# A 256-step recurrence on TensorE and ScalarE: the four block products of every second step in another order

## The chip, the cores and the metric

The kernel runs on one core of one Trainium2 chip. The metric is the device time of one execution in microseconds (us). TensorE (PE) multiplies, and its weight loads are a row of their own in the profile (PEld); ScalarE (ACT) evaluates tanh; VectorE (DVE) prepares inputs and adds outputs; SyncE's queue (SP) issues most transfers.

## What is computed

Two layers on x of 32 sequences, 256 steps and 256 features. In the first the transform and its inverse cancel up to a gate, so that the kernel computes x1 = x * (2 + gate). The second is a plain recurrence, and it is where the time goes:

```
h = silu(q_pool @ W1.T + b1);  gate = sigmoid(h @ W2.T + b2)
x = x + (v + a)                      # = x * (2 + gate)
next_h = tanh(prev_h @ Wh + xw)      # xw = x @ Wx + b, 256 steps in turn
x = x + h_t
```

Each step needs the whole h of the step before it: 256 features for 32 sequences.

## The kernel before

**Layout.** Features lie on the partitions, in two halves of 128. A step's argument z has half 0 and half 1, called m in the code; the h of the step before has half 0 and half 1, called k. z half m is bias + Wx part + sum over k of Wh[k, m] * h[k]. One step's recurrent work is thus four blocks (k, m): `recur(s, k, m, h)`. Each is issued by `by_columns` as four products on 32 columns of the array; a float32 product becomes two weight loads and two matmuls, so that a block is 8 of each in the trace.

**Names in the trace.** z half 0 lies in the tensors `bank_e`, half 1 in `bank_l`. A row `bank_e<-h_ring,wh_sb` is therefore block (0,0) or (1,0), and `bank_l<-h_ring,wh_sb` is block (0,1) or (1,1). In the text they are called e0, e1 (h half 0 and 1 into z half 0) and l0, l1 (into z half 1).

**Loop.** `TURN` is four steps; 64 turns run on PE with steps s = 0 to 3. Loop step s reads h of ring slot s and makes z of slot (s+1) mod 4. Before the four blocks of a step, `fill(s, turn)` issues work that does not need h: bias and input products for steps ahead (nothing at s = 0; at the others rows of the tiles `ones,b_sb` and `x_ring,wx_sb`). Everything on PE is issued in the order written; waits stand in that order too.

**Handshakes.** PE waits for `h_ready[s][k]` before the first block that reads h half k. The last matmul of block (1, m) increments `z_whole[m]`. ScalarE waits for `z_whole[0]`, writes tanh of half 0 into `h_ring`, then waits for `z_whole[1]` and does half 1 (line 178). In every second step it also waits for an output addition (`out_ready`) of long before. VectorE waits for h half 1 (`h_ready[..][1]`), adds outputs and scales the next inputs (`input_ready`), for which `fill` waits.

Of the kernel before, what the change touches and what calls it, by code (L numbers as in the profile page):

```python
# [14 lines left out]
def build(nc, x, x_first, w1_cond, w2, wx, wh, b_rows, out):  # L15
    CHUNKS, HALVES, N = x.shape[1:]
    D = HALVES * P
    B = w1_cond.shape[2] - D - 2
# [5 lines left out]
    TURN, PART = 4, 2  # L24
# [3 lines left out]
    with ExitStack() as ctx:  # L28
        def sb(name, shape, dt=F32):
            return ctx.enter_context(nc.sbuf_tensor(name, shape, dt))  # L30

        def sem(name):
            return ctx.enter_context(nc.semaphore(name))
# [30 lines left out]
        h_ring = sb("h_ring", [P, HALVES, TURN * B])  # L64
# [20 lines left out]
        def z_of(s, m, steps=1):  # L85
            part, of = divmod(s, PART)
            return bank_l[part][of][:, 0:B] if m else bank_e[part][:, of * B:(of + steps) * B]
# [23 lines left out]
        z_whole = [sem(f"z_whole_{m}") for m in range(HALVES)]  # L111

        h_ready = [[sem(f"h_ready_{s}{m}") for m in range(HALVES)] for s in range(TURN)]
# [68 lines left out]
        def _(pe):  # L182
# [8 lines left out]
            def by_columns(out, weights, moving, start=False, stop=False, columns=32):  # L191
                for q in range(0, P, columns):
                    done = nc.tensor.matmul(out[q:q + columns], weights[:, q:q + columns], moving,  # L193
                                            start=start, stop=stop, skip_group_check=True)
                return done
# [5 lines left out]
            def gate_product(layer, k, m, w_t, operand):  # L201
                return by_columns(z_ps[layer][m], w_t[:, k, m * P:(m + 1) * P], operand[:, k, :],
                                  start=(k == 0), stop=(k == HALVES - 1), columns=64)
# [11 lines left out]
            def lay_input(s, steps, k, m, columns=32):  # L215
                return by_columns(z_of(s, m, steps), wx_sb[:, k, m * P:(m + 1) * P],
                                  x_ring[:, k, s * B:(s + steps) * B], columns=columns)


            def recur(s, k, m, h, columns=32):  # L220
                return by_columns(z_of(s, m), wh_sb[:, k, m * P:(m + 1) * P], h, stop=(k == HALVES - 1),
                                  columns=columns)
# [8 lines left out]
            for m in range(HALVES):  # L231
                for k in range(HALVES):
                    if m == 0:
                        pe.wait_ge(w1_loaded[k], DMA)
                    done = gate_product(0, k, m, w1_t, cond_t)
                done.then_inc(z1_product, 1)
            keep_warm(1)
            for k in range(HALVES):
# [3 lines left out]
                for m in range(HALVES):  # L242
                    done = gate_product(1, k, m, w2_t, silu)
# [12 lines left out]
            for k in range(HALVES):  # L256
# [3 lines left out]
                for m in range(HALVES):  # L260
                    done = lay_input(0, 1 if m else 2, k, m, columns=64)
# [9 lines left out]
            def fill(s, turn):  # L271
                if s == 1:
                    pe.wait_ge(input_ready[1], turn)
                    for m in range(HALVES):
                        lay_bias(2, 2 - m, m)
                        lay_input(2, 2 - m, 0, m)
                        lay_input(2, 2 - m, 1, m)
                if s == 2:
                    lay_bias(3, 1, 1)
                    lay_input(3, 1, 0, 1)  # L280
                    lay_input(3, 1, 1, 1)
                    lay_bias(0, 2, 0)
                    pe.wait_ge(input_ready[0], turn)
                    lay_input(0, 2, 0, 0)
                if s == 3:
                    lay_input(0, 2, 1, 0)
                    for at in range(PART):
                        lay_bias(at, 1, 1)
                        lay_input(at, 1, 0, 1)
                        lay_input(at, 1, 1, 1)  # L290
# [10 lines left out]
            with nc.Fori(1, TURNS + 1, engines=only_pe, head_slot={pe.engine: 6}) as turn:  # L301
                for s in range(TURN):
                    fill(s, turn)
                    for k in range(HALVES):
                        pe.wait_ge(h_ready[s][k], turn)
                        for m in range(HALVES):
                            done = recur((s + 1) % TURN, k, m, h_ring[:, k, s * B:(s + 1) * B])
                            if k == HALVES - 1:
                                done.then_inc(z_whole[m], 1)

        @block.vector
        def _(dve):
# [124 lines left out]
```

## Time and profile before

| what | value |
|---|---|
| median of 3 runs | 197.54 us (197.27 to 198.22) |
| profiled execution, own time | 197.27 us |
| its span, first to last instruction | 195.3 us |
| outside the span | 1.97 us |
| granted TensorE clock over the span | 1.000 |

The profiled execution is the lowest of the three. Starts in the timeline are given to 0.01 us. The end of a matmul is a modelled value; starts of weight loads and of activations are recorded.

### The profile page before, as it was taken

The numbers are of one execution on the slowest core, as the hardware profiler recorded it, in microseconds if no ns is written. First come the engines' busy times: TensorE is split into PE (matmuls) and PEld (weight loads), VectorE is DVE, ScalarE is ACT, GpSimd is POOL, SyncE is SP. The second block draws the span as 40 slices with busy tenths as digits, with TensorE's granted clock in tenths as the row PEclk, the third lists the DMA queues.
The fourth block names the chain that finished last, engine by engine and source line by source line (L and its number), as shares of the span: only waits on it lengthen the run. The fifth ranks groups of instructions, "written<-read, shape, count | busy, mean of one in ns | idle before, by whom it ended". The sixth has DMA issues, their size and how long they took to land.

```text
span 195.3 us, 33383 instructions
## 1 busy us (share of the span) xinstructions
PE 176.3 (90%) x15962; PEld 164.9 (84%) x15962; DVE 97.3 (50%) x395; ACT 76.8 (39%) x518; POOL 0.5 (0%) x5
## 2 busy tenths in 40 slices
PE   5799999999999999999999999999999999999995
PEld 3788898898888889889888888988988888898895
DVE  0545546545555554654555555465455555546543
ACT  3234443344433444334443344433444334443342
POOL 1000000000000000000000000000000000000000
PEclk9999999999999999999999999999999999999999
DMA  6419999402020110202002020200202020020212
GB/s 201 132 42 371 414 409 412 187 0 107 0 107 2 45 64 0 107 0 107 0 22 87 0 109 0 107 0 2 107 0 107 0 107 2 0 109 0 107 54 54
DMA packets 7105, 17.98 MB, mean 92 GB/s; under 512 B 1459, under 2 KB 2867, under 8 KB 7094
## 3 DMA queue, kind: packets, MB, share of 16 engines
q1 hardware_dynamic: 6656, 17.32, 23.6%
q10 hardware_dynamic: 438, 0.55, 0.8%
q14 instruction: 9, 0.07, 0.1%
q8 instruction: 2, 0.03, 0.1%
HBM read 9.48 MB, written 8.39 MB: 91 GB/s over the span
## 4 chain that ended last, share of the span: by engine, by line
PE 87%; ACT 7%; DMA 2%; issue 2%; SPq 0%
PE bank_e L193 49%; PE bank_l L193 38%; ACT h_ring L178 7%; DMA w_t<-in_w 2%; SPq L129 0%
## 5 line engine op out<-in xcount | busy, mean ns | idle before, releaser
L193 PE MATMUL bank_e<-h_ring,wh_sb 128*32 128x32 f32 x4096 | 103.1, 200 | 14.1 <-ACT h_ring L178 14.1
L193 PE MATMUL bank_l<-h_ring,wh_sb 128*32 128x32 f32 x4096 | 99.2, 196 | 0.0
L193 PEld LDWEIGHTS bank_e<-h_ring,wh_sb 128*32 128x32 f32 x4096 | 75.6, 109 | 23.8 <-ACT h_ring L178 21.1
L178 ACT ACTIVATE h_ring<-bank_e 128x32 f32<-128x32 f32 x256 | 50.6, 198 | 111.1 <-PE bank_e L193 111.1
L339 DVE TENSOR_TENSOR x<-x,h_ring 128x128 f32<-128x128 f32 x129 | 37.6, 291 | 86.3 <-ACT h_ring L178 86.3
L193 PE MATMUL bank_l<-x_ring,wx_sb 128*32 128x32 f32 (+1 forms) x4112 | 79.7, 199 | 0.0
L193 PEld LDWEIGHTS bank_l<-h_ring,wh_sb 128*32 128x32 f32 x4096 | 77.3, 111 | 0.0
L193 PE MATMUL bank_e<-x_ring,wx_sb 128*32 128x64 f32 (+1 forms) x2056 | 73.9, 227 | 0.0
L193 PEld LDWEIGHTS bank_l<-x_ring,wx_sb 128*32 128x32 f32 (+1 forms) x4112 | 61.9, 110 | 0.0
L193 PE MATMUL bank_l<-ones,b_sb 128*32 128x32 bf16 (+1 forms) x1026 | 53.9, 180 | 0.0
L178 ACT ACTIVATE h_ring<-bank_l 128x32 f32<-128x32 f32 x256 | 50.3, 197 | 0.0
L193 PEld LDWEIGHTS bank_e<-x_ring,wx_sb 128*32 128x32 f32 (+1 forms) x2056 | 45.1, 109 | 0.0
L193 PEld LDWEIGHTS bank_l<-ones,b_sb 128*32 128x32 bf16 (+1 forms) x1026 | 38.2, 97 | 0.0
L326 DVE TENSOR_TENSOR x<-x,g_t 128x128 f32<-128x128 f32 x126 | 36.3, 288 | 2.2
L326 DVE TENSOR_TENSOR x_ring<-x,g_t 128x128 f32<-128x128 f32 x126 | 35.9, 285 | 0.9 <-ACT h_ring L178 0.9
L193 PE MATMUL bank_e<-ones,b_sb 128*32 128x64 bf16 x512 | 29.5, 194 | 0.0
L193 PEld LDWEIGHTS bank_e<-ones,b_sb 128*32 128x32 bf16 x512 | 17.6, 97 | 0.0
L161 ACT ACT_TABLE_LOAD x1 | 1.3, 1283 | 3.3 <-issue 3.3
L185 PE MATMUL bank_e<-ones 128*128 128x512 bf16 (+1 forms) x4 | 1.5, 525 | 1.0 <-DVE ones L342 1.0
L347 DVE SCALAR_TENSOR_TENSOR silu<-gate_bank,w_t,sig_z 128x32 f32<-128x32 f32 x2 | 0.4, 251 | 3.8 <-ACT sig_z L164 3.8
L193 PEld LDWEIGHTS bank_l<-silu,w_t 128*64 128x64 f32 x16 | 1.0, 222 | 1.6 <-DVE silu L347 1.6
L193 PEld LDWEIGHTS gate_bank<-w_t 128*64 128x64 f32 x16 | 1.0, 215 | 1.5 <-DMA w_t<-in_w_cond 1.5
(31 smaller groups left out, 14.1 us busy)
## 6 DMA issues: line engine op xcount, KB each, us to landing
x<-in_x SPq DMA_DIRECT2D x15, 512.0 KB, 9.3
out_dram<-x SPq DMA_DIRECT2D x15, 512.0 KB, 3.5
w_t<-in_w SPq DMA_DIRECT2D x1, 256.0 KB, 4.8
wx_sb<-in_wx SPq DMA_DIRECT2D x1, 256.0 KB, 5.1
wh_sb<-in_wh ACTq DMA_DIRECT2D x1, 256.0 KB, 4.4
x<-in_x SPq DMA_DIRECT2D x1, 256.0 KB, 3.1
out_dram<-x SPq DMA_DIRECT2D x1, 256.0 KB, 2.4
w_t<-in_w_cond ACTq DMA_DIRECT2D x1, 145.0 KB, 3.0
```

The lines of the kernel that those rows point to most:

```text
L161: nc.scalar.activation(table_t[:], ones[:, 0:1], ACT.Sigmoid)
L178: nc.scalar.activation(h_ring[:, m, s * B:(s + 1) * B], z_of(s, m), ACT.Tanh)\
L185: nc.tensor.matmul(idle_ps[:, 0:columns], ones[:], ones[:, 0:1].to_broadcast([P, columns]), start=True, stop=True)
L193: done = nc.tensor.matmul(out[q:q + columns], weights[:, q:q + columns], moving, start=start, stop=stop, skip_group_check=True)
L326: return nc.vector.tensor_tensor(own if in_place else by_steps(x_ring[:, :, of_turn]), raw, g_t[:].unsqueeze(2).to_broadcast([P, HALVES, P ...
L339: nc.vector.tensor_tensor(x1[:, c, :, cols], x1[:, c, :, cols], h_ring[:, :, s * B:(s + steps) * B], ALU.add).then_inc(out_ready, 1)
L347: nc.vector.scalar_tensor_tensor(out=silu[:, m, :], in0=z_ps[0][m], scalar=gate_b(0, m), in1=sig_z1[:, m, :], op0=ALU.add, op1=ALU.mult)\
```

## The change

In loop steps s = 1 and s = 3 the blocks are issued as (0,0), (1,0), (0,1), (1,1), that is e0, e1, l0, l1; in s = 0 and s = 2 they stay (0,0), (0,1), (1,0), (1,1), that is e0, l0, e1, l1. The wait for h half 1 still stands before the first block that reads it, so in steps 1 and 3 it stands before the second block and not before the third. Each z half is still counted whole at its block of k = 1.

```
-                    for k in range(HALVES):
-                        pe.wait_ge(h_ready[s][k], turn)
-                        for m in range(HALVES):
-                            done = recur((s + 1) % TURN, k, m, h_ring[:, k, s * B:(s + 1) * B])
-                            if k == HALVES - 1:
-                                done.then_inc(z_whole[m], 1)
+
+                    order = [(0, 0), (1, 0), (0, 1), (1, 1)] if s % 2 else [(0, 0), (0, 1), (1, 0), (1, 1)]
+                    for at, (k, m) in enumerate(order):
+                        if k not in [of for of, _ in order[:at]]:
+                            pe.wait_ge(h_ready[s][k], turn)
+                        done = recur((s + 1) % TURN, k, m, h_ring[:, k, s * B:(s + 1) * B])
+                        if k == HALVES - 1:
+                            done.then_inc(z_whole[m], 1)
```

PE's program, loop step s = 1 and the first rows of the fill of step 2 (`h_ready_10` is h of slot 1, half 0; one row is the products of one tile, so a block of four products is a row with a wait and one of x3). Before:

```order
L193 MATMUL bank_e1<-h_ring,wh_sb 32x32 [waits h_ready_10]
L193 MATMUL bank_e1<-h_ring,wh_sb 32x32 x3
L193 MATMUL bank_l10<-h_ring,wh_sb 32x32 x4
L193 MATMUL bank_e1<-h_ring,wh_sb 32x32 [waits h_ready_11]
L193 MATMUL bank_e1<-h_ring,wh_sb 32x32 x3
L193 MATMUL bank_l10<-h_ring,wh_sb 32x32 x4
L193 MATMUL bank_l11<-ones,b_sb 32x32 x4
```

and the same place with the change:

```order
L193 MATMUL bank_e1<-h_ring,wh_sb 32x32 [waits h_ready_10]
L193 MATMUL bank_e1<-h_ring,wh_sb 32x32 x3
L193 MATMUL bank_e1<-h_ring,wh_sb 32x32 [waits h_ready_11]
L193 MATMUL bank_e1<-h_ring,wh_sb 32x32 x3
L193 MATMUL bank_l10<-h_ring,wh_sb 32x32 x8
L193 MATMUL bank_l11<-ones,b_sb 32x32 x4
```

The wait for `h_ready_11` has moved ahead of block l0, and l0 and l1 now follow each other. Step 3 on PE, at the end of the turn, as one piece of the difference (`bank_e0` and `bank_l00` are z of slot 0):

```order
-L193 MATMUL bank_e0<-h_ring,wh_sb 32x32 x4
-L193 MATMUL bank_l00<-h_ring,wh_sb 32x32 x4
-L193 MATMUL bank_e0<-h_ring,wh_sb 32x32 x4
-L193 MATMUL bank_l00<-h_ring,wh_sb 32x32 x4
+L193 MATMUL bank_e0<-h_ring,wh_sb 32x32 x8
+L193 MATMUL bank_l00<-h_ring,wh_sb 32x32 x8
```

The same blocks in the same number stand there; only l0 and e1 have changed places. Steps 0 and 2 and every other engine's program are as before.

## Rows read from the trace of the kernel before

**Rows 1.** The page: span, busy time by engine, chain by engine

```profile
span 195.3 us, 33383 instructions
PE 176.3 (90%) x15962; PEld 164.9 (84%) x15962; DVE 97.3 (50%) x395; ACT 76.8 (39%) x518; POOL 0.5 (0%) x5
...
PE 87%; ACT 7%; DMA 2%; issue 2%; SPq 0%
```

**Rows 2.** Waits: who waited for whom, us in total, times, longest

```profile
ACT h_ring L178 <- PE bank_e L193: 111.1, 256, 2.0
DVE x L339 <- ACT h_ring L178: 86.3, 128, 0.9
PEld bank_e L193 <- ACT h_ring L178: 21.1, 63, 0.4
```

**Rows 3.** Timeline of ACT: start us, duration, engine, line, tiles, [idle before]

```profile
96.55 0.20 ACT L178 ACTIVATE h_ring<-bank_e 128x32 f32<-128x32 f32 x1 [0.43 <-PE bank_e L193]
...
101.58 0.20 ACT L178 ACTIVATE h_ring<-bank_e 128x32 f32<-128x32 f32 x1 [0.43 <-PE bank_e L193]
101.67 0.20 ACT L178 ACTIVATE h_ring<-bank_l 128x32 f32<-128x32 f32 x1
102.29 0.20 ACT L178 ACTIVATE h_ring<-bank_e 128x32 f32<-128x32 f32 x1 [0.43 <-PE bank_e L193]
102.39 0.20 ACT L178 ACTIVATE h_ring<-bank_l 128x32 f32<-128x32 f32 x1
103.01 0.20 ACT L178 ACTIVATE h_ring<-bank_e 128x32 f32<-128x32 f32 x1 [0.43 <-PE bank_e L193]
103.11 0.20 ACT L178 ACTIVATE h_ring<-bank_l 128x32 f32<-128x32 f32 x1
...
107.32 0.20 ACT L178 ACTIVATE h_ring<-bank_e 128x32 f32<-128x32 f32 x1 [0.43 <-PE bank_e L193]
```

**Rows 4.** Timeline of PEld: step 0, its next fill's last rows, step 1

```profile
101.82 0.16 PEld L193 LDWEIGHTS bank_e<-h_ring,wh_sb 128*32 128x32 f32 x8 [0.33 <-ACT h_ring L178]
101.88 0.16 PEld L193 LDWEIGHTS bank_l<-h_ring,wh_sb 128*32 128x32 f32 x8
101.94 0.17 PEld L193 LDWEIGHTS bank_e<-h_ring,wh_sb 128*32 128x32 f32 x8
102.01 0.17 PEld L193 LDWEIGHTS bank_l<-h_ring,wh_sb 128*32 128x32 f32 x8
102.07 0.14 PEld L193 LDWEIGHTS bank_e<-ones,b_sb 128*32 128x32 bf16 x4
...
102.37 0.26 PEld L193 LDWEIGHTS bank_l<-x_ring,wx_sb 128*32 128x32 f32 x16
102.54 0.16 PEld L193 LDWEIGHTS bank_e<-h_ring,wh_sb 128*32 128x32 f32 x8
102.60 0.17 PEld L193 LDWEIGHTS bank_l<-h_ring,wh_sb 128*32 128x32 f32 x8
102.66 0.16 PEld L193 LDWEIGHTS bank_e<-h_ring,wh_sb 128*32 128x32 f32 x7
```

**Rows 5.** Timeline of PEld: end of the fill behind step 1, step 2

```profile
103.03 0.19 PEld L193 LDWEIGHTS bank_e<-x_ring,wx_sb 128*32 128x32 f32 x8
103.26 0.16 PEld L193 LDWEIGHTS bank_e<-h_ring,wh_sb 128*32 128x32 f32 x8
```

**Rows 6.** Timeline of PEld: end of the fill behind step 2, step 3

```profile
101.11 0.11 PEld L193 LDWEIGHTS bank_e<-h_ring,wh_sb 128*32 128x32 f32 x1
101.11 0.11 PEld L193 LDWEIGHTS bank_l<-x_ring,wx_sb 128*32 128x32 f32 x1
...
101.24 0.11 PEld L193 LDWEIGHTS bank_e<-h_ring,wh_sb 128*32 128x32 f32 x1
```

**Rows 7.** Timeline of DVE: the scalings that fill waits for

```profile
101.39 0.28 DVE L326 TENSOR_TENSOR x_ring<-x,g_t 128x128 f32<-128x128 f32 x1
...
101.92 0.28 DVE L326 TENSOR_TENSOR x_ring<-x,g_t 128x128 f32<-128x128 f32 x1
```

## The prediction

> **What bounds the kernel now.** I read the page first, then the table of waits, then the timelines of ACT and of the weight loads around one turn. The page shows PE busy 90% of the span and 87% of the chain [rows 1], which looks like a kernel bound by PE's throughput. The waits say otherwise. ACT waited 256 times, once a step, for z half 0, 111.1 us in all; PE's weight loads waited for ACT only 63 times, once a turn [rows 2]. Both views are fooled by the fill: PE always has something to do while ACT works, except before step 0, where no fill stands.
>
> The timelines settle it. From the activation at 96.55 to that at 107.32 lie 15 steps: 10.77 / 15 = 0.718 us a step [rows 3]. Step 0, which finds PE idle for 0.33 us, takes as long as the others. So the step is a loop of latencies through both engines, and the fill fits into it. The loop, with A0 and A1 for the starts of tanh of half 0 and half 1:
>
> - A0 at 101.58, e0's first weight load at 101.82; A0 at 102.29, load at 102.54 [rows 3, 4]: 0.25. Of that 0.20 is the activation, 0.05 the release.
> - e0 at 101.82, l0 at 101.88, e1 at 101.94, l1 at 102.01, the fill's first load at 102.07 [rows 4]: four blocks in 0.25, so 0.0625 a block, and e1 stands 0.12 behind e0.
> - e1 at 101.94, next A0 at 102.29 [rows 3, 4]: 0.35. e0 to the next A0 is 0.47 in steps 0 and 1.
>
> 0.25 + 0.12 + 0.35 = 0.72. Block l0 lies in this loop, between e0 and e1, though z half 0 does not need it. Next to it runs h half 1: A1 starts 0.09 or 0.10 behind A0 (three pairs: 0.09, 0.10, 0.10; mean 0.095) [rows 3]. With the same 0.25 from start to release, e1 could have started 0.095 behind e0. It starts at 0.12, so its wait is met and it has 0.025 to spare.
>
> **The change, part by part.** Nothing is added or removed: 16 products a step before and after, in the same tiles, and the same two waits.
>
> *Odd steps (1 and 3), what they gain.* e1 moves up from 0.12. PE could issue it at 0.0625, but h half 1 is there only at 0.095. PE stalls 0.03. By the issue of loads the gain is 0.12 - 0.095 = 0.025. There is a second way to count. Let the array itself be in order, with every load at least its 0.11 ahead of its product (the single loads) [rows 6]. Then e0 occupies it from 0.11 to 0.17, l0 to 0.235, and e1 from 0.235 before; after the change e1's loads start at 0.095, its products at 0.205: gain 0.03. The two bounds are 0.025 and 0.031 (half a block, if e1's delay behind e0 goes from two blocks to one and a half). I take the middle, 0.028. Queued behind the stalled e1 are l0, l1 and the fill. l0 was issued at 0.0625 and now goes at 0.095 + 0.0625 = 0.16, l1 at 0.22 where it was at 0.19; the fill starts 0.03 later.
>
> *Is there room for that?* Behind step 3 the fill is empty and PE idles 0.33 [rows 4]. Behind step 1 the fill's last eight loads begin at 103.03, take 0.19 with the last load's own 0.11 included, so the last one begins at about 103.11; step 2 begins at 103.26 [rows 5]. The room is 0.15. It shrinks by 0.03 for the stall and by 0.028 for the earlier h, to about 0.09. So neither odd step is held back by PE.
>
> *Even steps (0 and 2), what they lose.* After an odd step z half 1 is whole two blocks after z half 0, 0.125, and was whole one block after it, 0.0625. A1 stands 0.095 behind A0 now, more than the 0.0625, so ACT and not PE sets that distance; afterwards PE sets it, and A1 will stand about 0.125 behind A0. The next e1, in an even step, is issued 0.12 behind e0 and finds its h at 0.125. It loses 0 (the array count, where 0.12 + 0.11 = 0.23 stands against 0.125 + 0.11 = 0.235, within the reading) to 0.007. I take 0.003. This is why only every second step can have the new order: the even step uses up the lateness of half 1 behind its own l0 and hands on A1 at 0.095 again.
>
> *The fills behind even steps* have no room: behind step 0 the sixteen loads from 102.37 last 0.26, so the last begins at 102.52, and e0 of step 1 follows at 102.54 [rows 4]; behind step 2 the last fill load stands at 101.11 beside e0 of step 3 at 101.11 [rows 6]. An even step cannot become shorter than 0.718 without meeting that. It does not: only the odd ones shorten, and a later e1 in an even step moves the fill and A0 alike.
>
> *VectorE.* Its scaling at 101.39 ends at 101.67 and feeds the fill from 102.07 [rows 4, 7], 0.40 early; the one at 101.92 ends at 102.20 and feeds loads at 103.03 [rows 5], 0.8 early. h half 1 comes up to 0.03 later relative to half 0. Covered, cost nothing; without that cover the cost would be at most the 0.03.
>
> **Sum.** z of steps 1 to 255 is made by 255 loop steps, of them 127 odd and 128 even. 127 x -0.028 + 128 x 0.003 = -3.56 + 0.38 = -3.2 us. Against the profiled execution's own 197.27 this gives 194.1. That execution lies 0.27 under the median of the runs, so for a median 194.3. The bounds of the sum: -127 x 0.031 = -3.9 and -127 x 0.025 + 128 x 0.007 = -2.3, so 193.6 to 195.2.
>
> **A rule against the row.** A0 to A1 is 0.095 where the activation's record is 0.20 long [rows 3], so two overlap by half. The Trainium skill's page "Perfetto Trace Analysis", section "Optimizing Scalar/DVE Operations", says that an operation's profiled latency is about twice its engine-busy time, because the write acknowledgement overlaps with the next instruction; half of 0.20 is the distance seen, so by that rule ACT sets it and the slack of half 1 is real. The page "TensorE: Matmul & The Clock Gate", Part 3, section "The mechanism", says that TensorE pulls weight loads ahead of products in flight. A stalled e1 can't have its loads pulled ahead of e0's products. If that exposed a whole load of 0.11 that is hidden now, an odd step would lose 0.11 - 0.03 = 0.08 and the kernel 10 us. The trace speaks against it: step 0 starts from an idle array and step 1 behind a running fill, and from e0 to the next A0 both take 0.47 [rows 3, 4].
>
> **Rivals.**
>
> *A late release (slower).* That h half 1 is there 0.095 behind e0 rests on the 0.05 from the end of an activation to the load, seen only for half 0 at the head of a step. PE never waited for half 1 in this trace. If the release is d later when PE stalls between two blocks, the odd step changes by -0.028 + d. A1's lateness meets the same wait in the even step, which changes by 0.003 + d. A pair changes by -0.025 + 2d: it decides at d = 0.0125, and with d = 0.03 the kernel is 128 x 0.035 = 4.5 us slower, 202.0; with d = 0.02, 199.5. For it: 12 ns is little. Against: 0.25 from A0 to the load was the same behind an idle PE and behind a fill that ended 0.02 before [rows 3, 4]. Chance 0.13.
>
> *Half 1 is late for the even steps (about no change).* l1 at 102.01 to A1 at 102.39 is 0.38, e1 to A0 0.35. If the 0.38 is what half 1 always needs, A1 comes 0.155 behind A0 after an odd step. The even e1 loses 0.155 - 0.12 = 0.035, a pair -0.028 + 0.035 = +0.007, in all +0.9: 198.4. Against: 0.095 where the blocks stand 0.0625 apart is just what a busy ACT would give. Chance 0.11.
>
> *The place of e1 is not what sets A0 (no change).* In step 3 e1 starts 0.13 behind e0 (101.11 to 101.24) and A0 still comes at 101.58, 0.47 behind e0 [rows 3, 6]. Something of 0.01 is thus not told by the starts of loads. If e0 to A0 were fixed by the number of products issued before it in some other way, nothing would be won: 197.5. Against: 8 products fewer stand before z half 0's last. Chance 0.1.
>
> *The full block is won (faster still).* If e1 went at 0.0625, 127 x 0.0625 = 7.9 us would go, 189.6. It needs h half 1 0.03 sooner than ACT delivers it. Chance 0.02.
>
> **How the numbers follow.** The likeliest case, the sum, has 0.64: 194.3, its own range 193.4 to 195.5. Leaving out the late release beyond about 0.01 and the full block, the range that holds 8 in 10 is 193.3 to 198.0. Within 0.5% of 197.54, about what a measurement of this kernel can tell from no change, lies 196.55 to 198.53: the two no-change rivals, 0.2 with a part of the small d. Faster: 0.66. Slower: 0.14.
>
> **What the profile after will show.** The steps alternate: A0 to A0 over an odd step about 0.69, over an even step 0.72. In steps 1 and 3 e1's first load stands 0.09 to 0.10 behind e0's, with a gap of 0.03 between the two, and the next A0 about 0.44 behind e0. A1 stands 0.12 to 0.13 behind A0 at the head of steps 0 and 2, and 0.09 to 0.10 at the head of 1 and 3. In even steps e1 stays at 0.12 to 0.13. The gap before step 0 grows little, that before step 2 falls from 0.15 to about 0.09. I am wrong if e1 in odd steps comes later than 0.11 behind e0 (late release), if A1 stands 0.15 or more behind A0 (half 1 late), or if e1 moves up and A0 does not follow.

## The result

The kernel with the change took 196.44 us (median of 8 runs, 196.01 to 196.92), the kernel before 197.49 (8 runs). The ratio on record is 0.9929, 95% interval 0.9913 to 0.9946: 1.4 us faster, within 1.07 and 1.72. The two medians alone lie 1.05 apart, just below that interval. Forecast were 194.3 and 3.2 us won. The direction was right and the size was more than double the truth.

The profiled execution took 196.62 us, its span 194.8. The page, as in [rows 1], and the first row of the table of waits, as in [rows 2]:

```profile
span 194.8 us, 33383 instructions
PE 176.0 (90%) x15962; PEld 167.4 (86%) x15962; DVE 98.2 (50%) x395; ACT 85.3 (44%) x518; POOL 0.5 (0%) x5
...
ACT h_ring L178 <- PE bank_e L193: 101.7, 256, 2.1
```

ACT is busy 85.3 us instead of 76.8 with the same number of instructions, each as long as before. Busy time is the time covered by at least one instruction, so the two tanhs of a step overlap less. That is the first sign of what happened. The timeline of ACT over one turn shows it, beside [rows 3] (start, duration, tiles, idle before):

```profile
101.71 0.20 ACT L178 ACTIVATE h_ring<-bank_e 128x32 f32<-128x32 f32 x1 [0.39 <-PE bank_e L193]
101.87 0.20 ACT L178 ACTIVATE h_ring<-bank_l 128x32 f32<-128x32 f32 x1
102.49 0.20 ACT L178 ACTIVATE h_ring<-bank_e 128x32 f32<-128x32 f32 x1 [0.42 <-PE bank_e L193]
102.58 0.20 ACT L178 ACTIVATE h_ring<-bank_l 128x32 f32<-128x32 f32 x1
103.17 0.20 ACT L178 ACTIVATE h_ring<-bank_e 128x32 f32<-128x32 f32 x1 [0.39 <-PE bank_e L193]
103.33 0.20 ACT L178 ACTIVATE h_ring<-bank_l 128x32 f32<-128x32 f32 x1
103.91 0.20 ACT L178 ACTIVATE h_ring<-bank_e 128x32 f32<-128x32 f32 x1 [0.39 <-PE bank_e L193]
104.01 0.20 ACT L178 ACTIVATE h_ring<-bank_l 128x32 f32<-128x32 f32 x1
104.59 0.20 ACT L178 ACTIVATE h_ring<-bank_e 128x32 f32<-128x32 f32 x1 [0.39 <-PE bank_e L193]
```

The steps alternate. From 102.49 to 103.17 (step 1) are 0.68 us, to 103.91 (step 2) 0.74, to 104.59 (step 3) 0.68; before, each took 0.718. A1 stands 0.16 behind A0 at the head of the even steps and 0.10 or 0.09 at the head of the odd ones. The timeline of weight loads, as in [rows 4], for step 1 (a row of x16 is two blocks) and for a step 2:

```profile
102.74 0.25 PEld L193 LDWEIGHTS bank_e<-h_ring,wh_sb 128*32 128x32 f32 x16
102.89 0.23 PEld L193 LDWEIGHTS bank_l<-h_ring,wh_sb 128*32 128x32 f32 x16
...
100.54 0.16 PEld L193 LDWEIGHTS bank_e<-h_ring,wh_sb 128*32 128x32 f32 x8
100.59 0.17 PEld L193 LDWEIGHTS bank_l<-h_ring,wh_sb 128*32 128x32 f32 x8
100.70 0.16 PEld L193 LDWEIGHTS bank_e<-h_ring,wh_sb 128*32 128x32 f32 x8
100.75 0.16 PEld L193 LDWEIGHTS bank_l<-h_ring,wh_sb 128*32 128x32 f32 x8
```

In step 1 the l blocks begin 0.15 behind e0, two blocks (0.125) and a stall. In step 2 e1 begins 0.16 behind e0 and not 0.12: it waits for the late half 1.

From here on numbers to 0.001 are medians of the starts that the trace records for steps 12 to 249. Odd steps take 0.678 (0.040 won), even ones 0.744 (0.026 lost). A pair wins 0.015 (by means rather than medians). 127 pairs give -1.9 us. One thing more stands against it: in 15 turns of this execution, every fourth one, step 0 took longer, about 0.78 in 14 of them, as from 101.71 to 102.49 above, because e0 came 0.06 late. These turns cost about 0.035 each, 0.5 us. Both together are -1.4, as measured. Read directly from the traces, steps 12 to 249 together are 1.30 us shorter, which is 1.4 for all 255.

The two profiled executions differ by less, 197.27 to 196.62, because their starts differ, in a part where both kernels have the same program. The last weight loads before the loop, before and with the change:

```profile
9.40 0.34 PEld L193 LDWEIGHTS bank_l<-x_ring,wx_sb 128*64 128x64 f32 x8
...
10.07 0.57 PEld L193 LDWEIGHTS bank_l<-x_ring,wx_sb 128*64 128x64 f32 x8
```

The first tanh stands at 9.53 before and at 10.18 with the change, and the first step takes 0.750 and 1.036. In the kernels below, too, the first four steps take up to about 1 us more than before without an order that asks for it. What makes a start slow isn't shown. So a difference below 1 us between two single executions is read from steps 12 to 249 and not from the total.

### The profile page after: what moved, and what is told of

The parts are those of the page before. It is cut to its first block, busy times and chain, and to the rows that moved or that the text cites. A ratio compares the mean times of both kernels' runs of the same rounds, so it can differ in the third digit from the quotient of the medians.

```text
span 194.8 us, 33383 instructions
## 1 busy us (share of the span) xinstructions
PE 176.0 (90%) x15962; PEld 167.4 (86%) x15962; DVE 98.2 (50%) x395; ACT 85.3 (44%) x518; POOL 0.5 (0%) x5
## 4 chain that ended last, share of the span: by engine, by line
PE 86%; ACT 7%; issue 3%; DMA 3%; SPq 0%
PE bank_e L193 48%; PE bank_l L193 38%; ACT h_ring L178 7%; DMA w_t<-in_w 3%; SPq L129 0%
## 5 line engine op out<-in xcount | busy, mean ns | idle before, releaser
L193 PE MATMUL bank_e<-h_ring,wh_sb 128*32 128x32 f32 x4096 | 98.6, 204 | 13.5 <-ACT h_ring L178 13.5
L193 PE MATMUL bank_l<-h_ring,wh_sb 128*32 128x32 f32 x4096 | 91.2, 196 | 0.0
L193 PEld LDWEIGHTS bank_e<-h_ring,wh_sb 128*32 128x32 f32 x4096 | 71.5, 108 | 20.2 <-ACT h_ring L178 20.1
L193 PE MATMUL bank_l<-x_ring,wx_sb 128*32 128x32 f32 (+1 forms) x4112 | 81.0, 200 | 0.0
L193 PE MATMUL bank_e<-x_ring,wx_sb 128*32 128x64 f32 (+1 forms) x2056 | 71.0, 224 | 0.0
L193 PEld LDWEIGHTS bank_l<-h_ring,wh_sb 128*32 128x32 f32 x4096 | 69.8, 113 | 0.0
L193 PEld LDWEIGHTS bank_l<-x_ring,wx_sb 128*32 128x32 f32 (+1 forms) x4112 | 64.5, 111 | 0.0
L193 PE MATMUL bank_l<-ones,b_sb 128*32 128x32 bf16 (+1 forms) x1026 | 51.7, 180 | 0.0
L193 PEld LDWEIGHTS bank_e<-x_ring,wx_sb 128*32 128x32 f32 (+1 forms) x2056 | 43.2, 110 | 0.0
L193 PEld LDWEIGHTS bank_l<-ones,b_sb 128*32 128x32 bf16 (+1 forms) x1026 | 34.3, 98 | 0.0
```

## Experiments

Short diffs are against the kernel with the change unless another is named. "Ratio" is to the kernel before, with its 95% interval; a single time stands beside the kernel before on the same chip.

**One odd step at a time.**

```
-  order = [...new...] if s % 2 else [...old...]
+  order = [...new...] if s == 1 else [...old...]        # second kernel: if s == 3
```

> The new order in step 1 alone. Theory A (read from the trace after the change): a new-order step takes 0.678 us instead of 0.718, and the ordinary step behind it 0.744, because tanh of half 1 then starts 0.159 behind that of half 0 and not 0.125. A turn changes by -0.040 + 0.026 = -0.014, 64 turns by -0.9 us: 196.6 against 197.5, ratio about 0.9955. Rival B (the prediction's sum, 0.028 won and 0.003 lost a pair): -1.6 us, ratio 0.992.

> The new order in step 3 alone. Theory A: step 3 takes 0.678; step 0 behind it 0.744, in every fourth turn 0.779, because the loop's turn-round on PE, hidden before, now comes out behind a step 3 that ends later. A turn changes by -0.040 + 0.035 = -0.005, 64 turns by -0.35 us, ratio 0.998. Rival B: the turn-round has nothing to do with it and step 3 is worth as much as step 1, -0.9 us, ratio 0.9955; then the late starts in every fourth turn would not show here alone and would show also where only step 1 is changed.

Step 1 alone: ratio 0.9954 (0.9930 to 0.9978). Step 1 takes 0.677, step 2 behind it 0.744, the others 0.718, as theory A said. Step 3 alone: ratio 0.9956 (0.9936 to 0.9977). Step 3 takes 0.678, step 0 behind it 0.744 in most turns and 0.76 to 0.78 in 9 of 60, without a pattern of four. The ratios can't tell the two kernels apart; in the traces steps 12 to 249 are 0.99 us shorter with step 1 changed and 0.72 with step 3. The time came out as rival B had it, but late starts do show with step 3 alone, which B had ruled out. e0 of step 0 comes 0.263 behind A0 instead of 0.248 in all turns, which costs nothing where e1 waits for half 1 anyway; it costs only where e0 is later than that. With step 1 alone changed no step 0 follows a new order, and e0 is not late there. That the loop's turn-round on PE is what makes it late is inferred from the place; why the late turns come every fourth time in the kernel with the change is open. In both kernels the price is paid in the step behind the new order, not in the new-order step.

**The new order in every step, and in the even ones.**

```
-  order = [...new...] if s % 2 else [...old...]
+  order = [...new...]                                   # second kernel: if s % 2 == 0
```

> The new order in all four steps. Theory A (half 1 needs 0.033 more than half 0 from its last product to its tanh): tanh of half 1 stands 0.159 behind that of half 0 in every step, the second block waits for it, and each step takes 0.248 + 0.159 + 0.337 = 0.744: +6.6 us over 255 steps, 204, ratio 1.033. Rival B (the prediction's: half 1 follows half 0 by the two blocks' 0.125): each step takes 0.248 + 0.125 + 0.337 = 0.710: -2.0 us, 195.5, ratio 0.990.

> The new order in steps 0 and 2 and the old in 1 and 3. Tests whether the fill has room: behind steps 0 and 2 the fill's loads end 0.01 to 0.02 before the next step. Theory A with the fill as a bound: tanh comes 0.04 earlier, the fill ends 0.03 later, so the next step's first block starts at least 0.05 late, and a pair takes 0.678 + 0.774 = 1.452 instead of 1.436: +2.0 us, 199.5, ratio 1.010. Rival B, PE's stream has hidden room there: a pair takes 0.678 + 0.744 = 1.422, and no turn-round stands behind a new-order step: -1.8 us, 195.7, ratio 0.991.

Every step: ratio 1.031 (1.028 to 1.035), each step 0.744, A1 0.159 behind A0 in all of them. Theory A's sum holds: 0.248 + 0.159 + 0.337. With the prediction's 0.125 in that sum a step would take 0.710 and the kernel be 2 us faster than before; it is 6 us slower.

Even steps: ratio 1.0083 (1.0056 to 1.0111). Steps 0 to 3 take 0.678, 0.760, 0.677, 0.785. What room there is behind step 2 is what the rows of this kernel show, first ACT and then the weight loads:

```profile
100.19 0.20 ACT L178 ACTIVATE h_ring<-bank_e 128x32 f32<-128x32 f32 x1 [0.39 <-PE bank_e L193]
```

```profile
100.37 0.24 PEld L193 LDWEIGHTS bank_l<-x_ring,wx_sb 128*32 128x32 f32 x15
100.51 0.11 PEld L193 LDWEIGHTS bank_e<-h_ring,wh_sb 128*32 128x32 f32 x1
100.52 0.11 PEld L193 LDWEIGHTS bank_l<-x_ring,wx_sb 128*32 128x32 f32 x1
```

e0 of step 3 begins at 100.51, 0.32 behind A0 instead of 0.25, among the fill's last loads. The fill has no room there, as the prediction read from [rows 6]. Behind step 0 it had some: e0 of step 1 comes 0.256 behind A0, 0.008 late and not 0.05. That step 1 takes 0.760 all the same and not 0.744 is because its e1 begins 0.262 behind A1 instead of 0.248; why is open.

**Part of a block moved.** The block l0 is cut by its four column products: the first ones stay ahead of e1, and only the rest stands behind it.

```
+  cut = 64 if s % 2 else P        # others: 64 in every step; 96 in every step
+  order = [(0, 0, 0, P), (0, 1, 0, cut), (1, 0, 0, P), (0, 1, cut, P), (1, 1, 0, P)]
```

> In steps 1 and 3 only half of block l0 (two of its four column products) moves behind e1: e0, half l0, e1, half l0, l1. Theory A (tanh of half 1 stands the spacing of the two last products plus 0.033 behind that of half 0, at least 0.094): the half block fills the 0.03 in which PE stalled, e1 still starts at 0.094, a step 1 or 3 takes 0.68; the last products of the halves lie 0.094 apart instead of 0.125, so half 1's tanh stands 0.127 behind and not 0.159, and steps 0 and 2 take 0.718 to 0.726 instead of 0.744. About -0.034 a pair, -3.8 us with some 0.5 for the turn-round: 193.8, ratio 0.981. Rival B, half 1's tanh comes at 0.159 whenever e1 stands before the end of l0: no better than the change, ratio 0.993.

> The half block moved in all four steps. Theory A: half 1's tanh stands 0.094 + 0.033 = 0.127 behind half 0's in every step and e1 waits for it; a step takes 0.248 + 0.127 + 0.34 = 0.715, -0.7 us, ratio 0.996. Rival B, half 1 always at 0.159: 0.744 a step, ratio 1.033.

> One of the four column products of l0 moved behind e1 in all four steps (e0, three quarters of l0, e1, the last quarter, l1). Theory A: e1 could be issued at 0.109, half 1's tanh stands 0.078 + 0.033 = 0.111 behind half 0's, so the two meet and nothing stalls; a step takes about 0.70 to 0.71. Behind step 2, where the fill has only about 0.005 of room, the next step starts about 0.01 late. -2.5 to -4 us, ratio 0.980 to 0.987. Rival B, half 1 at 0.159: 0.744 a step, ratio 1.033.

Ratios 0.9968 (0.9951 to 0.9985), 1.0143 (1.0097 to 1.0189) and 0.9974 (0.9954 to 0.9993). The times of none come near their expectations, of either theory. ACT and the weight loads of the first kernel, step 1 and its successor:

```profile
100.33 0.20 ACT L178 ACTIVATE h_ring<-bank_e 128x32 f32<-128x32 f32 x1 [0.40 <-PE bank_e L193]
...
101.04 0.20 ACT L178 ACTIVATE h_ring<-bank_e 128x32 f32<-128x32 f32 x1 [0.42 <-PE bank_e L193]
101.17 0.20 ACT L178 ACTIVATE h_ring<-bank_l 128x32 f32<-128x32 f32 x1
```

```profile
100.58 0.16 PEld L193 LDWEIGHTS bank_e<-h_ring,wh_sb 128*32 128x32 f32 x8
100.63 0.15 PEld L193 LDWEIGHTS bank_l<-h_ring,wh_sb 128*32 128x32 f32 x4
100.69 0.16 PEld L193 LDWEIGHTS bank_e<-h_ring,wh_sb 128*32 128x32 f32 x8
100.74 0.20 PEld L193 LDWEIGHTS bank_l<-h_ring,wh_sb 128*32 128x32 f32 x10
```

Half of l0 went out of the way, four weight loads instead of eight, yet e1 still begins 0.108 behind e0 in step 1 and 0.121 in step 3. It isn't held by its wait: it stands 0.263 behind A1 in step 1, where a waiting block stands 0.248 behind. A0 stands 0.463 behind e0's load where it was 0.470. With only a quarter moved it is 0.463 too. A block that is moved whole gives 0.429. So for A0 it matters little how much of l0 stands before e1, and much whether any does. The reading that fits: the four column products of a block use four column groups of the array at once, and z half 0 is whole when its last group is. A group with a product of l0 before e1's is as late as before. The Trainium skill's page "TensorE: Matmul & The Clock Gate", Part 3, says that column tiles run concurrently; the 0.463 of both kernels fits it. The reading is inferred from these two, not measured by itself.

This is where theory A missed: it let A0 come earlier by the part moved. Its distances between the tanhs were right. It had 0.127, 0.127 and 0.111 for A1 behind A0; measured are 0.126, 0.126 and 0.109 (0.116 at the head of step 1 in the last). Behind e1 stand half of l0 or a quarter of it, and l1: 0.094 or 0.078 by the count of products, and 0.03 more. A cut that cost a full turn of 0.0625 again behind e1 would give 0.125 for the quarter too, and doesn't fit 0.109. With the cut in every step the fill of step 3 again has no room: e0 of step 3 comes 0.281 behind A0 with half a block and 0.262 with a quarter, and that step takes 0.748 and 0.730. The other steps take 0.712 to 0.722 with half a block, where 0.715 was expected, and 0.712 or 0.713 with a quarter.

**Where the extra 0.03 of half 1 comes from.** After step 1 in the new order the last products of the two halves start 0.127 apart (medians of the recorded matmul starts), but the tanhs 0.159. Four kernels put other products into step 1, ahead of or between its l blocks.

```
   e0, e1, <fill of step 2>, l0, l1            # e5
   e0, e1, <bias block>, l0, l1                # e9
   e0, e1, l0, <bias block>, l1                # e10
   e0, e1, <bias and one input block>, l0, l1  # e11
```

> The kernel with the change, but in step 1 blocks l0 and l1 are issued behind the whole fill, so that z half 1 is whole some 0.55 us after half 0, when ScalarE has long ended the tanh of half 0. Measures what the last product of half 1 needs to its tanh. After the change it is 0.295 from the recorded start of that matmul, against 0.264 for half 0. Theory A1, ScalarE is still busy with half 0's tanh when half 1 becomes whole: with an idle ScalarE half 1 takes 0.264 too. Theory A2, half 1 needs 0.03 more by itself (its bank or its place behind other products): 0.295 again. In both the kernel is some 27 us slower, since step 2 waits for half 1 about 0.43 longer.

> The kernel with the change, but in step 1 the fill's first four products (one bias block, 0.031 of issue) stand between e1 and l0, so that z half 1 is whole 0.156 behind half 0 instead of 0.125, while ScalarE is still in half 0's tanh (0.197 long). Theory A1 (half 1 pays 0.033 more while half 0's tanh runs) and theory A2 (it always pays it) both give 0.190 from tanh to tanh at the head of step 2, and a step 2 of 0.775. If ScalarE could start only at fixed places (0.094, 0.126, 0.159) it would be 0.19 too. Rival C, half 1's extra 0.033 is the array's own, because l0 and l1 write the same place of PSUM back to back: 0.190 here, but see the next run.

> The same four bias products between l0 and l1 of step 1. Rival C (back-to-back writes of the same place cost 0.033): the bias products fill that gap, tanh of half 1 stays 0.159 behind half 0's and step 2 at 0.744. Theories A1 and A2: 0.190 and 0.775, as with the products before l0.

> The bias block and one input block (0.031 + 0.0625) between e1 and l0 of step 1, so that z half 1 is whole 0.219 behind half 0, by when half 0's tanh (0.197) has ended. Theory A1 (the extra is paid only behind a running tanh): tanh to tanh 0.22, step 2 0.80. Theory A2 (half 1 always needs 0.033 more): 0.252, step 2 0.837.

The times were 215.4, 198.07, 199.34 and 202.65 us, beside 197.9 for the kernel before with the first and 197.7 with the last three. Tanh to tanh at the head of step 2: 0.449, 0.192, 0.193 and 0.259. The pair e9 and e10 settles rival C, which had 0.159 for e10: bias products between l0 and l1 don't shorten anything, so two products in a row on one place of PSUM are not the cause. e5 and e11 seemed to favour an idle ScalarE: half 1's tanh stood 0.242 and 0.260 behind its last product. They don't decide it. In both, that product stands in a slower part of the stream, where also half 0's distance was 0.235 in step 3 of the kernel before against 0.269 in step 2. The next kernel leaves TensorE's program alone.

```
-  for m in range(HALVES):
+  halves = (1, 0) if s == 2 and t < T - TURN else (0, 1)
+  for m in halves:
```

> The kernel with the change, its products untouched; only ScalarE, at the head of step 2, takes half 1 first and half 0 behind it. Half 1's tanh then starts on an idle ScalarE, from the same last product in the same stream as before. After the change it starts 0.296 behind the recorded start of that product. Theory A1 (the extra 0.03 is paid only behind a running tanh): 0.264. Theory A2 (half 1 always needs it): 0.296 again. Half 0's tanh follows about 0.094 later in both, so step 1 gets about 0.19 to 0.22 longer, some 12 to 14 us in all, less what step 2 wins because half 1 is there at once: e1 no longer waits, 0.744 becomes 0.72.

It took 210.29 us. ACT at the head of step 2, and step 1's first loads:

```profile
99.98 0.20 ACT L179 ACTIVATE h_ring<-bank_e 128x32 f32<-128x32 f32 x1 [0.42 <-PE bank_e L194]
...
100.82 0.20 ACT L179 ACTIVATE h_ring<-bank_l 128x32 f32<-128x32 f32 x1 [0.55 <-PE bank_l L194]
100.91 0.19 ACT L179 ACTIVATE h_ring<-bank_e 128x32 f32<-128x32 f32 x1
```

```profile
100.23 0.25 PEld L194 LDWEIGHTS bank_e<-h_ring,wh_sb 128*32 128x32 f32 x16
```

ScalarE had been idle for 0.55, and half 1's tanh still starts 0.59 behind e0's first load, as with the change (102.74 to 103.33). To the last product it is 0.295 again. The theory of the running tanh (A1 in the expectations) falls. The run shows another thing: half 0 had long been whole, and its tanh starts 0.09 behind the other's. That is ScalarE's own distance between two tanhs, and it was read rightly from [rows 3].

Two kernels then changed the halves over in step 1, with the same order of tanhs as the last one.

```
+  if s == 1: order = [(0, 1), (1, 1), (0, 0), (1, 0)]   # e13: l0, l1, e0, e1
+  if s == 1: order = [(0, 1), (0, 0), (1, 1), (1, 0)]   # e14: l0, e0, l1, e1
```

> Step 1 mirrored: l0, l1, e0, e1 on TensorE, and ScalarE takes half 1 first at the head of step 2. The last run left that half 1's tanh stands 0.295 behind the recorded start of its last product even on an idle ScalarE, half 0's 0.263. Theory D (position: the half that is finished second, two blocks later, pays 0.03): now half 1 stands 0.263 behind its product and half 0 0.295, and the second tanh starts 0.159 behind the first. Theory E (the half's own: its bank or its semaphore): half 1 still 0.295, half 0 0.263, so the first tanh comes 0.03 later than in the kernel with the change and the second 0.094 to 0.1 behind it. The kernel's time is that of the change under D, 196 to 197.

> Step 1 in the old order but with the halves changed over: l0, e0, l1, e1, and half 1's tanh first. Theory D: half 1 stands 0.47 behind the first block's load, as half 0 does in the old order, and half 0's tanh 0.094 behind. Theory E: half 1 stands 0.50 behind the first block's load, and half 0's tanh 0.094 behind.

The first, loads and tanhs:

```profile
101.14 0.25 PEld L194 LDWEIGHTS bank_l<-h_ring,wh_sb 128*32 128x32 f32 x16
101.29 0.23 PEld L194 LDWEIGHTS bank_e<-h_ring,wh_sb 128*32 128x32 f32 x16
```

```profile
101.57 0.20 ACT L179 ACTIVATE h_ring<-bank_l 128x32 f32<-128x32 f32 x1 [0.39 <-PE bank_l L194]
101.73 0.20 ACT L179 ACTIVATE h_ring<-bank_e 128x32 f32<-128x32 f32 x1
102.45 0.20 ACT L179 ACTIVATE h_ring<-bank_e 128x32 f32<-128x32 f32 x1 [0.52 <-PE bank_e L194]
```

Half 1, now first, starts 0.43 behind its first load and 0.263 behind its last product; half 0, now second, 0.159 later and 0.296 behind its own. In the other kernel half 1 stands 0.470 behind the first load. Of the two theories D holds and E falls: the extra doesn't belong to half 1, it changes sides with the order. The forecast of the first kernel's time, 196 to 197, was wrong, 205.12 us; the second, for which no time was forecast, took 203.19. Half 1's early tanh doesn't help step 2, whose first block reads half 0: with that half second, e0 waits for it, and from the first tanh of one step to the first of the next is 0.88 (101.57 to 102.45).

How far theory D goes has a limit. The 0.295 behind the last product's recorded start is seen where step 1 runs in the order e0, e1, l0, l1 or its mirror. With bias products put in it is 0.286 (e9, e10), with a bias and an input block 0.260 (e11), and with half of l0 ahead of e1 in every step it is 0.262 (e7), the same as the first half's 0.263, although half 1 is finished second there too, its last product 0.127 behind. The recorded starts and the count of products disagree on e7. The count fits all of them (e5 wasn't counted): 0.0625 for a block of four recurrent or input products and 0.031 for a bias block behind e1, and 0.033, give 0.158, 0.189, 0.189, 0.252, 0.127 and 0.111 for the change, e9, e10, e11, e7 and e8, where 0.159, 0.192, 0.193, 0.259, 0.126 and 0.109 were measured. A rival is that the 0.033 isn't the second half's loss but what the first half wins because its last block stands right behind a stall. e6 and e8 speak against it: their e1 is not held by its wait in step 1, and the distance still has the 0.033. No kernel was made for this question, none puts a stall before the second half's own last block.

## Why the prediction was right in direction and wrong in size

- **The loop of latencies, and l0 in it: right.** Taking l0 out of odd steps shortens them, and the fill hid nothing of it. (The sum's own terms add up to 194.4 for a median, where 194.3 was written.)
- **What an odd step wins, 0.025 to 0.031: 0.040 measured**, above both bounds. e1 stood 0.092 behind e0, as the forecast said (0.095), 0.027 earlier than before. The rest is that A0 follows e1's load by 0.337 and not by 0.351. The even steps show the same 0.337 when e1 stalls, so it belongs to a block that starts behind a stall. Before, e1's loads ran ahead of its products: the first product's recorded start stood 0.030 behind its load, and 0.002 behind it after a stall. That 0.35 held some of that lead is the reading; how much isn't shown.
- **The step that failed:** "ACT and not PE sets that distance; afterwards PE sets it, and A1 will stand about 0.125 behind A0." It stands 0.159 behind. The term that was mis-sized is the loss of an even step. The sum held 0.003 for an even step; e1 waits there until 0.159, 0.040 later than at 0.119, and with the 0.014 of the stalled block the step loses 0.026. 128 x 0.026 is 3.3 us where 0.4 was set down. The even step does not use up the lateness of half 1 for nothing; it pays most of it. With the new order in all steps the same distance decides between 2 us won and the 6 us lost that were measured.
- **The cause of the failure.** In the trace before, the distance between the halves' tanhs was 0.094, and two things explained it: ScalarE's own least distance, which is real, and an extra of 0.03 for the half that is finished second, which would give 0.0625 + 0.03. One number hid the other. The rival "half 1 is late for the even steps" named 0.155 and got chance 0.11; the row that spoke for it, 0.38 from l1 to A1 against 0.35 from e1 to A0, was seen, and set aside because a busy ACT explained 0.095 as well. The rival was right about the place and the distance, and wrong in the price of the pair (+0.007, measured -0.015), because both kinds of step gained the 0.014.
- **The late release: absent.** The wait between two blocks is released as fast as the one at the head: e1 begins 0.247 behind A1, and e0 0.248 behind A0.
- **Room behind odd steps: right** for step 1. Behind step 3, where the prediction saw 0.33 of idle PE and set down nothing, e0 of step 0 comes 0.264 behind A0 instead of 0.248, and about 0.31 in 14 turns, which cost about 0.5 us of the profiled execution. That term was missing.
- **VectorE covered: right**; no wait on it came up.
- **What stays open:** why the second half's tanh comes 0.03 later than the products between account for. It isn't a running tanh, the half's bank or semaphore, or the place of PSUM written twice. It goes with being finished second by the count of products; the recorded starts of the last products show it in some orders only.

No version tried had a lower ratio than the kernel with the change, though its interval and those of the one-step versions overlap. Over steps 12 to 249 it is the shortest too.

## What to carry to other kernels

A distance that equals a floor is no proof that the floor sets it: look whether the second of two chains has slack, by its own latency from issue to consumer, before a delay is hung on it. When two halves feed each other in turn, time won for the first is handed to the second, and the price shows one step later; a change in every step would have told its size at once. And moving part of a block need not win its share: here half or a quarter of l0 won 0.007 of the 0.041 that the whole block won.

## What the runs showed of the hardware

- With the blocks of step 1 as e0, e1, l0, l1, or mirrored, the tanh of the half that is finished second starts 0.295 behind the recorded start of its last product, that of the first 0.263, whichever half it is and whether ScalarE is idle or not. In other orders the second half's was 0.242 to 0.286 (e5, e7, e9, e10, e11).
- The distance of the two tanhs was 0.033 more than the count of products between them, within 0.007, from one and a quarter to three and a half blocks of 0.0625, with a bias block counted as half of one. e5 wasn't counted so.
- Two tanhs of 128x32 started 0.094 apart at least, with the second's operand long whole (e12).
- A block whose wait stalls costs less from its first load to its consumer (0.337) than one in a running stream (0.351).
- Recorded matmul starts carry an error of that size: in steps 1, 2 and 3 of the kernel before, A0 stood 0.258, 0.269 and 0.235 behind the last product's recorded start, and 0.470 behind the first load in all of them. In these steps the loads were the steady mark.
- Cutting a block into two and two column products gave 0.463 instead of 0.470, the same as three and one.
